# Node pass of a graph layer: on GpSimd the gather of aggregated rows is issued before the second norm's operation instead of behind it

## The chip, the cores and the metric

The kernel runs on one core of one Trainium2 chip. Its five engines (TensorE or PE, VectorE or DVE, ScalarE or ACT, GpSimd or POOL, SyncE or SP) run rows of instructions of their own and meet only at semaphores. The metric is the device time of one execution in microseconds (us), the median of several runs.

## The reference, cut to what matters

Inputs are 50000 nodes of 768 numbers and 25000 edges, sorted by destination.

```python
x = x + gnn(layernorm(x), src, dst, W, attn_l, attn_r, W_res)
x = x + ffn(layernorm(x), ...)

def gnn(h, src, dst, ...):                 # 12 heads of 64
    ft = einsum('nhd,od->nho', h, W)
    e = leaky_relu(a1[src] + a2[dst])      # then a softmax over the edges of a node
    agg = segment_sum(alpha[:, :, None] * ft[src], dst)
    res = einsum('nhd,od->nho', h, W_res)
    return relu(agg + res)

def ffn(x, ...):                           # 768 -> 96 -> 768; six class tokens aside
    return gelu(x @ W1 + b1) @ W2 + b2
```

An edge pass computes `agg` for nodes that have edges, and a node pass computes everything that every node needs: first norm, residual product, sum with `agg`, relu, second norm, feed-forward.

## The kernel before

The edge pass (to about 1150 us) leaves rows of `agg` in a scratch tensor in HBM, `agg_scratch`, and for every node the number of its row in `row_scratch`; nodes without edges have a number out of bounds, which the gather skips. The change doesn't touch the edge pass.

The node pass handles 392 units of 128 nodes, one in each iteration t of a loop that is written out in full (two turns of 196 and a drain). Each engine has its own copy of the loop, and in iteration t each step works on a unit that lies a fixed lag behind: the constants L_BASE = 3, L_RES = 4, L_Y = 5, L_SQ = 6, L_N2 = 9, L_T2 = 10, L_UP = 12, L_DOWN = 14, L_OUT = 15. Within an iteration the order of the code is the order of the engine's row; between engines only semaphores order things. The steps:

- SyncE loads the rows of x (`in_x`), their numbers `nrow` and a transposed copy (`in_x_cols`), and stores the output.
- ScalarE takes sums for the first norm (L644, L682), L665 the square sum for the second norm, L656 `t_hi`, a copy of the transposed second norm out of PSUM, and gelu.
- GpSimd, iteration t: **base** (L554) writes minus mean times weight sums times r_n into a slot of `g_ring`, for unit t-3. **n2** (L566) writes the second norm of unit t-9 into one of two buffers. **gather** (L574) is an indirect DMA that copies the rows of `agg_scratch` of unit t-3 over base in the slot, for the nodes that have one. In every even iteration **r_n** (L582) follows, the inverse roots for two units, out of `ve_n` from VectorE.
- TensorE, iteration t: the transposes of n2 of unit t-10 (L711), the up product (L845), the down product (L857) and the residual product of unit t-4 (L866), which waits for y of unit t-5.
- VectorE, iteration t: output sum (L1176), **z1** (L1187) for unit t-5, which adds the gathered slot and waits for the gather's landing (`d_g`) and the residual product, **y** (L1192), `t_lo` (L1199) behind `t_hi`, and in even iterations `ve_n` (L1210 to L1212), which releases r_n.

So a pair of iterations on GpSimd has two base, two n2, two gathers and one r_n. Base of the next odd iteration waits for r_n (`s_rn`), and so does its n2; the gather waits for base of the same iteration (`s_base`) and for `nrow` (`d_x`). n2 also waits for the transposes of two units before (`s_tp2`). In the first iterations, 3 to 8, there is no n2 yet.

Of the kernel before, what the change touches and what calls it, by code (L numbers as in the profile page):

```python
# [18 lines left out]
PAIR = 2  # L19
U = 196  # L20
XR = 14
GR = 7
NT = -(-N_NODES // (P * U)) * U
# [8 lines left out]
EP = EC * P  # L32
# [22 lines left out]
L_BASE = 3  # L55
# [16 lines left out]
def turns(eng, n, drain):  # L72


    yield 0
    yield 1
    if n > 2:
        with eng.Fori(2, n) as b:
            yield b
    for b in range(drain):  # L80
        yield n + b


def settle(eng):

    eng.nop(nofuse=True)


def exists(t, n):

    return not isinstance(t, int) or 0 <= t < n


def at_least(eng, sem, value):

    if not isinstance(value, int) or value > 0:
        eng.wait_ge(sem, value)


def gnn_ffn_kernel(nc, x, x_cols, edges, dst_next, dst_prev, dst_ends, chunk_base, sel_heads,  # L100
# [9 lines left out]
    with ExitStack() as ctx:  # L110
        def sb(name, shape, dt=f32):
            return ctx.enter_context(nc.sbuf_tensor(name, shape, dt))

        def sem(name):
            return ctx.enter_context(nc.semaphore(name))


        agg_d = nc.dram_tensor("agg_scratch", [EP, D], f32).ap()
# [7 lines left out]
        def part(lo, *shape, rows=P):  # L126
            size = 1
            for s in shape:
                size *= s
            flat = arena[0:rows, lo:lo + size]  # L130
            if len(shape) == 2:
                return flat.rearrange("p (a b) -> p a b", b=shape[1])
            if len(shape) == 3:
                return flat.rearrange("p (a b c) -> p a b c", b=shape[1], c=shape[2])
            return flat
# [12 lines left out]
        g_ring = part(16128, GR, D)  # L148
# [94 lines left out]
        nrow = sb("nrow", [P, XR], i32)  # L243
# [101 lines left out]
        d_x = [sem(f"d_x{u}") for u in range(XR // PAIR)]  # L345
        d_out = [sem(f"d_out{u}") for u in range(XR // PAIR)]
        d_xt = [sem(f"d_xt{u}") for u in range(GR)]
        d_g = [sem(f"d_g{u}") for u in range(GR)]
# [4 lines left out]
        s_base = sem("s_base")  # L353
# [138 lines left out]
        @block.gpsimd  # L492
        def _(pool):
            pool.wait_ge(d_rowinit, 16)

            for b in turns(pool, NB, 1):
                for i in range(BODY):
                    c = BODY * b + i
                    k = i % G
                    if exists(c, EC):  # L500
                        e = i // G
                        if k == 0:
                            pool.wait_ge(s_es, 2 * b + e + 1)
                        at_least(pool, s_tr, NBLK * (c - BODY + 1))
                        settle(pool)
                        pool.indirect_dma_start(xs_ring[:, i, :], None, x,
                                                bass.IndirectOffsetOnAxis(e_slot[:, e, k, 0:1], 0)).then_inc(d_ge[i], 16)
                        at_least(pool, s_sc, c - BODY)
                        settle(pool)
                        pool.indirect_dma_start(xd_ring[:, i, :], None, x,  # L510
                                                bass.IndirectOffsetOnAxis(e_slot[:, e, k, 1:2], 0)).then_inc(d_ge[i], 16)
                        at_least(pool, s_sum, c - BODY - L_SUM + L_TR + 1)
                        settle(pool)
                        pool.indirect_dma_start(row_d, bass.IndirectOffsetOnAxis(e_slot[:, e, k, 2:3], 0),
                                                e_slot[:, e, k, 3:4], None, bounds_check=NP - 1, oob_is_err=False)\
                            .then_inc(d_scat[e], 16)
                    gp = 2 * b + (i - 11) // G
                    if k == 11 % G and exists(gp, NG):
                        w = (i - 11) // G % 2
                        pool.wait_ge(s_ve, gp + 1)  # L520
                        settle(pool)
                        pool.tensor_tensor(r_a[:, w, 0:2 * G:2], ve_a[:, w, 0:2 * G:2], half[:, 0:G], ALU.pow)\
                            .then_inc(s_rp, 1)
                    gq = 2 * b + (i - 12) // G
                    if k == 12 % G and exists(gq, NG):
                        w = (i - 12) // G % 2
                        pool.tensor_tensor(r_a[:, w, 1:2 * G:2], ve_a[:, w, 1:2 * G:2], half[:, 0:G], ALU.pow)\
                            .then_inc(s_rpd, 1)

            for u in range(AR):  # L530
                pool.wait_ge(d_agg[u], 16 * (EC // AR))
            pool.wait_ge(s_idx, 1)
            for n in range(2):
                pool.indirect_dma_start(o_first[:, n, :], None, agg_d,
                                        bass.IndirectOffsetOnAxis(idx_i[:, n:n + 1], 0)).then_inc(d_first, 16)
            pool.wait_ge(s_frow, NC)
            pool.wait_ge(d_last, 16)
            pool.wait_ge(d_first, 32)
            for n in range(2):
                pool.indirect_dma_start(agg_d, bass.IndirectOffsetOnAxis(idx_i[:, n:n + 1], 0),  # L540
                                        fix_rows[:, n, :], None).then_inc(d_fix, 16)
            pool.wait_ge(d_fix, 32)
            for b in turns(pool, NT // U, 1):
                for u in range(U):
                    t = b * U + u
                    tb_ = t - L_BASE
                    if exists(tb_, NT):
                        v = (u - L_BASE) % XR
                        w = (v // PAIR + 1) % (XR // PAIR)
                        g = (u - L_BASE) % GR  # L550
                        pool.wait_ge(s_rn, b * (U // PAIR) + (u - L_BASE) // PAIR + 1)
                        at_least(pool, s_z1, tb_ - GR + 1)
                        settle(pool)
                        pool.tensor_scalar(g_ring[:, g, :].rearrange("p (c f) -> p c f", f=P),  # L554
                                           csr_neg[:, None, :].to_broadcast([P, NC, P]),
                                           mv1[:, w, 2 * (v % PAIR):2 * (v % PAIR) + 1], r_n[:, w, v % PAIR:v % PAIR + 1],
                                           ALU.mult, ALU.mult).then_inc(s_base, 1)
                    ty = t - L_N2
                    if exists(ty, NT):
                        v = (u - L_N2) % XR  # L560
                        w = (v // PAIR + 4) % (XR // PAIR)
                        k = v % PAIR
                        pool.wait_ge(s_rn, b * (U // PAIR) + (u - L_N2) // PAIR + 4)
                        at_least(pool, s_tp2, ty - 1)
                        settle(pool)
                        pool.tensor_scalar(n2[:, v % 2, :], y_ring[:, v, :], nm_n[:, w, k:k + 1],  # L566
                                           r_n[:, w, PAIR + k:PAIR + k + 1], ALU.add, ALU.mult).then_inc(s_n2, 1)
                    if exists(tb_, NT):
                        v = (u - L_BASE) % XR
                        g = (u - L_BASE) % GR  # L570
                        pool.wait_ge(d_x[v // PAIR], 32 * (U // XR * b + (u - L_BASE) // XR + 1))
                        pool.wait_ge(s_base, tb_ + 1)
                        settle(pool)
                        pool.indirect_dma_start(g_ring[:, g, :], None, agg_d,  # L574
                                                bass.IndirectOffsetOnAxis(nrow[:, v:v + 1], 0),
                                                bounds_check=EP - 1, oob_is_err=False).then_inc(d_g[g], 16)
                    q = b * (U // PAIR) + u // PAIR
                    if u % PAIR == 0 and exists(q - 1, NQ + 3):
                        w = u // PAIR % (XR // PAIR)
                        pool.wait_ge(s_ven, q)  # L580
                        settle(pool)
                        pool.tensor_tensor(r_n[:, w, :], ve_n[:, w, :], half[:, 0:4], ALU.pow).then_inc(s_rn, 1)  # L582
# [728 lines left out]
```

## Time and profile before

| | us |
|---|---|
| median of 3 runs | 3027.69 |
| lowest, highest | 3019.7, 3028.32 |
| the profiled execution, its own time | 3026.71 |
| span of its instructions | 3024.9 |
| mean granted TensorE clock (share of full speed) | 0.975 |

The busy shares of the whole span are TensorE 92%, VectorE 86%, ScalarE 72%, GpSimd 70%. They mix an edge pass and a node pass; the node pass starts to write its steps at about 1250 us. The profile's engines are named PE (with PEld for its weight loads), DVE, ACT, POOL. A wait is put down to what came last by the profile, and where a row names an engine that had long been done, it was something else, as in the waits of base "for PE L711" of 0.2 us, which is the wait for its own r_n. DMA_INDIRECT on POOL is the issue of a gather; the time until the rows have landed is not part of it.

### The profile page before, as it was taken

The page shows a single profiled execution, that of the slowest core. Times are in us where ns is not written, and L with a number is a line of the kernel's source. Part 1 is how long each engine was busy: PE and PEld are TensorE (multiplying, and loading weights), DVE is VectorE, ACT ScalarE, POOL GpSimd, SP SyncE. Part 2 cuts the span into 40 slices and gives each one's busy share as a digit, 9 for nine tenths or more (in the row PEclk, how much of TensorE's full clock was granted, in tenths as well). Part 3 has the DMA queues.
Part 4 walks back from the last instruction along what each step waited for, and adds up shares of the span by engine and source line. Part 5 has one row for each costly group of instructions (what it writes and reads, how often), then busy time and mean ns, then how long its engine had stood idle before and what let it go on. Part 6 is the DMA issues. An engine that isn't in the chain of part 4 may idle for free. (4 is left out here: it accounts for less than half of the span.)

```text
span 3024.9 us, 67973 instructions
## 1 busy us (share of the span) xinstructions
PE 2794.6 (92%) x21300; PEld 2580.3 (85%) x21300; DVE 2601.7 (86%) x5435; ACT 2186.3 (72%) x4168; POOL 2123.3 (70%) x2027
## 2 busy tenths in 40 slices
PE   1989999999999995589999999999999999999998
PEld 1878888888888883488999999999989999999996
DVE  4678899999999976488999999999989999989995
ACT  0655566666666561388888888998988989989992
POOL 6755566666666720378888888888878888888882
PEclk9999999999999998599999999999999999999998
DMA  8999999888887733489888888888888888888873
GB/s 176 168 182 211 197 217 215 220 217 212 220 218 219 213 120 125 167 289 326 313 311 313 304 306 307 301 300 305 301 281 296 305 294 302 302 288 296 298 259 126
DMA packets 246631, 758.02 MB, mean 251 GB/s; under 512 B 78899, under 2 KB 81203, under 8 KB 246291
## 3 DMA queue, kind: packets, MB, share of 16 engines
q1 hardware_dynamic: 176644, 545.08, 51.2%
q0 software_dynamic: 69312, 209.33, 31.2%
q8 instruction: 123, 2.02, 0.3%
q14 instruction: 120, 0.98, 0.1%
q10 hardware_dynamic: 432, 0.62, 0.1%
HBM read 623.04 MB, written 232.17 MB: 283 GB/s over the span
## 5 line engine op out<-in xcount | busy, mean ns | idle before, releaser
L866 PE MATMUL ps<-wr_bd,arena 128*128 128x128 f32 x4704 | 608.1, 280 | 92.9 <-DVE arena L1192 85.3
L866 PEld LDWEIGHTS ps<-wr_bd,arena 128*128 128x128 f32 x4704 | 567.7, 194 | 113.5 <-issue 111.6
L1187 DVE SCALAR_TENSOR_TENSOR ps<-ps,r_n,arena 128x768 f32<-128x768 f32 x392 | 400.1, 1021 | 114.4 <-DMA arena<-agg_scratch,nrow 93.6
L574 POOL DMA_INDIRECT arena<-agg_scratch,nrow x392 | 438.9, 1120 | 77.6 <-issue 72.4
L656 ACT ACTIVATE t_hi<-ps 128x768 fp32r<-128x768 f32 x392 | 315.0, 804 | 176.3 <-PE ps L711 176.2
L554 POOL TENSOR_SCALAR arena<-csr_neg,mv,r_n 128x768 f32<-128x768 f32 x392 | 386.8, 987 | 50.6 <-PE ps L711 37.7
L613 ACT ACTIVATE arena<-ps 128x512 f32<-128x512 f32 x588 | 312.1, 594 | 138.5 <-PE ps L728 100.4
L1192 DVE SCALAR_TENSOR_TENSOR arena<-ps,arena 128x768 f32<-128x768 f32 x392 | 375.3, 957 | 13.4
L566 POOL TENSOR_SCALAR arena<-arena,nm_n,r_n 128x768 f32<-128x768 f32 x392 | 383.4, 978 | 0.6 <-POOL r_n L582 0.4
L644 ACT ACTIVATE arena<-arena,mv 128x768 f32<-128x768 f32 x392 | 367.7, 938 | 12.7
L1199 DVE TENSOR_TENSOR t_lo<-ps,t_hi 128x768 fp32r<-128x768 f32 x392 | 373.7, 953 | 2.9 <-ACT t_hi L656 2.6
L1176 DVE TENSOR_TENSOR arena<-arena,ps 128x768 f32<-128x768 f32 x392 | 369.8, 943 | 6.3 <-PE ps L857 6.1
L665 ACT ACTIVATE arena<-arena,s_st 128x768 f32<-128x768 f32 x392 | 363.8, 928 | 9.8 <-DVE arena L1192 9.8
L845 PE MATMUL ps<-t_hi,w_hi 128*96 128x256 f32 x1176 | 361.0, 307 | 0.0
L728 PE MATMUL ps<-ident,arena 128*128 128x128 f32 x2352 | 296.2, 277 | 50.9 <-issue 49.7
L582 POOL TENSOR_TENSOR r_n<-ve_n,half 128x4 f32<-128x4 f32 x199 | 205.8, 1034 | 187.7 <-DVE ve_n L1212 187.1
L728 PEld LDWEIGHTS ps<-ident,arena 128*128 128x128 f32 x2352 | 275.3, 143 | 71.3 <-issue 52.6
L510 POOL DMA_INDIRECT arena<-in_x,e_slot x196 | 190.7, 973 | 198.5 <-PE ps L774 111.0
L845 PE MATMUL ps<-t_lo,w_hi 128*96 128x256 f32 x1176 | 329.8, 280 | 0.0
L845 PE MATMUL ps<-t_hi,w_lo 128*96 128x256 f32 x1176 | 328.7, 280 | 0.0
L682 ACT ACTIVATE arena<-arena 128x768 f32<-128x768 f32 x392 | 326.0, 832 | 0.5
L711 PE MATMUL ps<-ident,arena 128*128 128x128 f32 x2352 | 323.2, 274 | 1.3 <-POOL arena L566 0.8
(201 smaller groups left out, 6556.7 us busy)
## 6 DMA issues: line engine op xcount, KB each, us to landing
arena<-in_x SPq DMA_DIRECT2D x196, 768.0 KB
arena<-in_x_cols SPq DMA_DIRECT2D x392, 384.0 KB
out<-arena SPq DMA_DIRECT2D x195, 768.0 KB, 5.6
agg_scratch<-arena SPq DMA_DIRECT2D x196, 384.0 KB
arena<-in_x,e_slot POOLq DMA_INDIRECT x392
arena<-agg_scratch,nrow POOLq DMA_INDIRECT x392
row_scratch<-e_slot POOLq DMA_INDIRECT x196
nrow<-row_scratch SPq DMA_DIRECT2D x196, 1.0 KB
```

The source lines that it names most:

```text
L554: pool.tensor_scalar(g_ring[:, g, :].rearrange("p (c f) -> p c f", f=P), csr_neg[:, None, :].to_broadcast([P, NC, P]), mv1[:, w, 2 * (v % ...
L566: pool.tensor_scalar(n2[:, v % 2, :], y_ring[:, v, :], nm_n[:, w, k:k + 1], r_n[:, w, PAIR + k:PAIR + k + 1], ALU.add, ALU.mult).then_inc( ...
L574: pool.indirect_dma_start(g_ring[:, g, :], None, agg_d, bass.IndirectOffsetOnAxis(nrow[:, v:v + 1], 0), bounds_check=EP - 1, oob_is_err=Fa ...
L644: nc.scalar.activation(junk[:, 0, :], x_ring[:, v, :], ACT.Square, bias=mv1[:, w, 2 * k:2 * k + 1], scale=-1.0, accum_out=q_st[:, w, k:k + ...
L665: nc.scalar.activation(junk[:, 1, :], y_ring[:, v, :], ACT.Square, bias=s_st[:, w, k:k + 1], scale=-float(D), accum_out=q_st[:, w, 2 + k:3 ...
L728: last = nc.tensor.transpose(ps[:, k, m % 4 * P:(m % 4 + 1) * P], src[:, v, m % NC * P:(m % NC + 1) * P], ident[:])
L845: last = nc.tensor.matmul(ps[0:HID, 6 + v, 0:PAIR * P], w[:, i, :], h[:, i, :], start=(i == 0 and n == 0), stop=(i == NC - 1 and n == 2))
L866: last = nc.tensor.matmul(pair(1)[:, i * P:(i + 1) * P], xt_ring[:, g, i * P:(i + 1) * P], wr_bd[:], start=True, stop=True)
L1176: V.tensor_tensor(y_ring[:, v, :], y_ring[:, v, :], pair(2), ALU.add).then_inc(s_o, 1)
L1187: V.scalar_tensor_tensor(pair(1), pair(1), r_n[:, w, k:k + 1], g_ring[:, g, :], ALU.mult, ALU.add).then_inc(s_z1, 1)
L1192: V.scalar_tensor_tensor(y_ring[:, v, :], pair(1), 0.0, x_ring[:, v, :], ALU.max, ALU.add, accum_out=s_st[:, w4, k:k + 1]).then_inc(s_y, 1)
L1199: V.tensor_tensor(t2_lo[:, v, :, f], pair(0).rearrange("p (c n) -> p c n", c=NC), t2_hi[:, v, :, f].bitcast(f32), ALU.subtract).then_inc(s ...
```

## The change

The six lines of code of the gather move up, from behind n2 to ahead of it. Nothing else changes. What was L574 (the gather) becomes L564, and n2 moves from L566 to L575.

```diff
                     if exists(tb_, NT):
                         ...
                         pool.tensor_scalar(g_ring[:, g, :].rearrange("p (c f) -> p c f", f=P),
                         ...
                                            ALU.mult, ALU.mult).then_inc(s_base, 1)
+                    if exists(tb_, NT):
+                        v = (u - L_BASE) % XR
+                        g = (u - L_BASE) % GR
+                        pool.wait_ge(d_x[v // PAIR], 32 * (U // XR * b + (u - L_BASE) // XR + 1))
+                        pool.wait_ge(s_base, tb_ + 1)
+                        settle(pool)
+                        pool.indirect_dma_start(g_ring[:, g, :], None, agg_d,
+                                                bass.IndirectOffsetOnAxis(nrow[:, v:v + 1], 0),
+                                                bounds_check=EP - 1, oob_is_err=False).then_inc(d_g[g], 16)
                     ty = t - L_N2
                     if exists(ty, NT):
                         ...
                         pool.tensor_scalar(n2[:, v % 2, :], y_ring[:, v, :], nm_n[:, w, k:k + 1],
                                            r_n[:, w, PAIR + k:PAIR + k + 1], ALU.add, ALU.mult).then_inc(s_n2, 1)
-                    if exists(tb_, NT):
-                        ...
-                        pool.indirect_dma_start(g_ring[:, g, :], None, agg_d,
-                        ...
```

On GpSimd, at the seam between the iterations without n2 and the first one with it, before:

```order
194 L554 TENSOR_SCALAR arena<-csr_neg,mv,r_n 128x768 [waits s_rn]
195 L574 DMA arena<-agg_scratch,nrow 128x768 [waits d_x2,s_base]
196 L582 TENSOR_TENSOR r_n<-ve_n,half 128x4 [waits s_ven]
197 L554 TENSOR_SCALAR arena<-csr_neg,mv,r_n 128x768 [waits s_rn]
198 L566 TENSOR_SCALAR arena<-arena,nm_n,r_n 128x768 [waits s_rn]
199 L574 DMA arena<-agg_scratch,nrow 128x768 [waits d_x3,s_base]
200 L554 TENSOR_SCALAR arena<-csr_neg,mv,r_n 128x768 [waits s_rn,s_z1]
```

and of the changed kernel, in the same place:

```order
194 L554 TENSOR_SCALAR arena<-csr_neg,mv,r_n 128x768 [waits s_rn]
195 L564 DMA arena<-agg_scratch,nrow 128x768 [waits d_x2,s_base]
196 L582 TENSOR_TENSOR r_n<-ve_n,half 128x4 [waits s_ven]
197 L554 TENSOR_SCALAR arena<-csr_neg,mv,r_n 128x768 [waits s_rn]
198 L564 DMA arena<-agg_scratch,nrow 128x768 [waits d_x3,s_base]
199 L575 TENSOR_SCALAR arena<-arena,nm_n,r_n 128x768 [waits s_rn]
200 L554 TENSOR_SCALAR arena<-csr_neg,mv,r_n 128x768 [waits s_rn,s_z1]
```

Without n2 (rows 194 and 195) the order base, gather is the same in both; from row 198 on gather and n2 have changed places.

On GpSimd, a pair of iterations once all steps stand there, from the base of an odd iteration to the r_n of the even one, before:

```order
204 L554 TENSOR_SCALAR arena<-csr_neg,mv,r_n 128x768 [waits s_rn,s_z1]
205 L566 TENSOR_SCALAR arena<-arena,nm_n,r_n 128x768 [waits s_rn,s_tp2]
206 L574 DMA arena<-agg_scratch,nrow 128x768 [waits d_x4,s_base]
207 L554 TENSOR_SCALAR arena<-csr_neg,mv,r_n 128x768 [waits s_rn,s_z1]
208 L566 TENSOR_SCALAR arena<-arena,nm_n,r_n 128x768 [waits s_rn,s_tp2]
209 L574 DMA arena<-agg_scratch,nrow 128x768 [waits d_x4,s_base]
210 L582 TENSOR_TENSOR r_n<-ve_n,half 128x4 [waits s_ven]
```

and of the changed kernel:

```order
204 L554 TENSOR_SCALAR arena<-csr_neg,mv,r_n 128x768 [waits s_rn,s_z1]
205 L564 DMA arena<-agg_scratch,nrow 128x768 [waits d_x4,s_base]
206 L575 TENSOR_SCALAR arena<-arena,nm_n,r_n 128x768 [waits s_rn,s_tp2]
207 L554 TENSOR_SCALAR arena<-csr_neg,mv,r_n 128x768 [waits s_rn,s_z1]
208 L564 DMA arena<-agg_scratch,nrow 128x768 [waits d_x4,s_base]
209 L575 TENSOR_SCALAR arena<-arena,nm_n,r_n 128x768 [waits s_rn,s_tp2]
210 L582 TENSOR_TENSOR r_n<-ve_n,half 128x4 [waits s_ven]
```

In each iteration the gather stands directly behind the base that it waits for, and n2 between it and the next base or r_n. The rows of the other engines are the same.

## Rows read from the trace of the kernel before

**Rows 1.** Page, costliest groups: busy us, mean ns | idle us before them, releaser.

```profile
L1187 DVE SCALAR_TENSOR_TENSOR ps<-ps,r_n,arena 128x768 f32<-128x768 f32 x392 | 400.1, 1021 | 114.4 <-DMA arena<-agg_scratch,nrow 93.6
L574 POOL DMA_INDIRECT arena<-agg_scratch,nrow x392 | 438.9, 1120 | 77.6 <-issue 72.4
```

**Rows 2.** Waits, 1278.88 to 2959.5 us: us in total, times, longest us.

```profile
POOL r_n L582 <- DVE ve_n L1212: 172.2, 187, 5.0
...
DVE ps L1187 <- DMA arena<-agg_scratch,nrow: 88.7, 98, 4.8
...
PE ps L866 <- DVE arena L1192: 65.9, 76, 4.8
```

**Rows 3.** Busy time by stretch, from the first n2 to the last gather.

```profile
core 0: us, PE busy (x) PEld busy (x) DVE busy (x) ACT busy (x) POOL busy (x), PEclk, DMA share, GB/s
1278.88:2959.50 1680.62, 1606.72 (x12676) 1538.06 (x12676) 1529.71 (x2694) 1489.60 (x3072) 1385.77 (x1350) 0.99 0.87 299
```

**Rows 4.** Timeline of POOL, mid node pass: start us, us, instruction, [idle before].

```profile
1997.78 1.09 POOL L574 DMA_INDIRECT arena<-agg_scratch,nrow  x1 [0.17 <-issue]
1999.65 1.04 POOL L582 TENSOR_TENSOR r_n<-ve_n,half 128x4 f32<-128x4 f32 x1 [0.78 <-DVE ve_n L1212]
2000.89 0.99 POOL L554 TENSOR_SCALAR arena<-csr_neg,mv,r_n 128x768 f32<-128x768 f32 x1 [0.21 <-PE ps L711]
2001.87 0.98 POOL L566 TENSOR_SCALAR arena<-arena,nm_n,r_n 128x768 f32<-128x768 f32 x1
2003.02 1.14 POOL L574 DMA_INDIRECT arena<-agg_scratch,nrow  x1 [0.17 <-issue]
2004.21 0.98 POOL L554 TENSOR_SCALAR arena<-csr_neg,mv,r_n 128x768 f32<-128x768 f32 x1
2005.19 0.97 POOL L566 TENSOR_SCALAR arena<-arena,nm_n,r_n 128x768 f32<-128x768 f32 x1
2006.33 1.11 POOL L574 DMA_INDIRECT arena<-agg_scratch,nrow  x1 [0.17 <-issue]
2008.74 1.03 POOL L582 TENSOR_TENSOR r_n<-ve_n,half 128x4 f32<-128x4 f32 x1 [1.31 <-DVE ve_n L1212]
```

**Rows 5.** Timeline of POOL in the iterations before n2 begins.

```profile
1258.88 1.09 POOL L574 DMA_INDIRECT arena<-agg_scratch,nrow  x1 [0.89 <-issue]
1260.00 1.05 POOL L582 TENSOR_TENSOR r_n<-ve_n,half 128x4 f32<-128x4 f32 x1
1261.23 0.98 POOL L554 TENSOR_SCALAR arena<-csr_neg,mv,r_n 128x768 f32<-128x768 f32 x1 [0.18 <-POOL r_n L582]
1263.07 1.14 POOL L574 DMA_INDIRECT arena<-agg_scratch,nrow  x1 [0.85 <-POOL arena L554]
1264.26 0.98 POOL L554 TENSOR_SCALAR arena<-csr_neg,mv,r_n 128x768 f32<-128x768 f32 x1
1266.09 1.11 POOL L574 DMA_INDIRECT arena<-agg_scratch,nrow  x1 [0.84 <-issue]
1267.45 1.04 POOL L582 TENSOR_TENSOR r_n<-ve_n,half 128x4 f32<-128x4 f32 x1 [0.26 <-DVE ve_n L1212]
```

**Rows 6.** Timeline of DVE, mid node pass.

```profile
2005.48 1.03 DVE L1187 SCALAR_TENSOR_TENSOR ps<-ps,r_n,arena 128x768 f32<-128x768 f32 x1 [0.88 <-DMA arena<-agg_scratch,nrow]
...
2007.42 0.95 DVE L1199 TENSOR_TENSOR t_lo<-ps,t_hi 128x768 fp32r<-128x768 f32 x1
...
2009.36 1.02 DVE L1187 SCALAR_TENSOR_TENSOR ps<-ps,r_n,arena 128x768 f32<-128x768 f32 x1
```

**Rows 7.** Timeline of PEld and ACT, mid node pass.

```profile
1999.86 0.69 PEld L711 LDWEIGHTS ps<-ident,arena 128*128 128x128 f32 x6
...
2000.82 0.82 ACT L656 ACTIVATE t_hi<-ps 128x768 fp32r<-128x768 f32 x1 [0.63 <-PE ps L711]
...
2003.96 0.69 PEld L711 LDWEIGHTS ps<-ident,arena 128*128 128x128 f32 x6
```

## What I expect of the change

> **What bounds the kernel now.** I read four views: the groups of the page, for what is long and what stands idle ahead of it; the waits of the node pass, for who waits for whom; the timeline of GpSimd (POOL), for how its instructions follow one another; and the same stretch on VectorE (DVE), ScalarE (ACT) and TensorE (PE). In the groups the reader is to see that z1 (L1187) is idle most often for the gather, and that the gather has an idle of its own [rows 1]. In the waits: GpSimd waits 172.2 us for VectorE at r_n, so GpSimd has slack today; VectorE waits 88.7 us in 98 places for a gather to land; TensorE waits 65.9 us for y (L1192), behind z1 [rows 2].
>
> The stretch in which base, n2 and gather all stand is iterations 9 to 394: 386 iterations, 193 pairs (r_n comes once a pair). It lasts 1680.62 us [rows 3], so **8.71 us a pair**. TensorE alone would need less: with no wait, the transposes of two iterations stand 4.10 us apart (1999.86 and 2003.96), 8.20 us a pair [rows 7]. The rest is a loop through the gather. The second gather of a pair starts 6.68 us after r_n (1999.65 to 2006.33) [rows 4], is needed at a z1 two iterations on, and from the start of z1 to the r_n behind it are 3.26 us (2005.48 to 2008.74) [rows 4, 6]. Two pairs must hold 6.68, the time L from gather start to landing, and 3.26. Where z1 waited, at 2005.48, its gather had started at 1997.78: L = 7.70 us less the release [rows 4, 6]. Two pairs of 8.71 ask for an L of 7.5, so landing time of the second gather and the 8.20 of TensorE share the bound. The first gather of a pair isn't the late one: it starts at 2003.02 and its z1, at 2009.36, shows no wait [rows 4, 6].
>
> **What the change does to GpSimd's row.** Instructions, waits and sizes stay; only the order within an iteration turns. Before, while n2 runs for 0.98 us, the gather's wait for s_base and its preparation run beneath it, and 0.17 us behind n2 it starts: 1.15 us after base ends [rows 4]. After, nothing lies between base and gather. The trace shows that case: in the first iterations n2 isn't there yet, and the gather stands right behind its base. There the idle time is **0.85 and 0.84 us** (1263.07 and 1266.09), and so in every pair before n2 begins [rows 5]. The same instruction with the same waits, so I take 0.84. The nearest other row is the 0.21 between r_n and a base that waits for it [rows 4]; it is my lower bound, and r_n and base are both compute operations, so it is the farther one. The upper is 1.15, if the gather doesn't start sooner at all; both gaps at that price would make the pair 9.82 and add 214 + 10 us, 3251. Since the gap behind base is the same instruction and lies at 0.84 to 0.89 in all rows of this kind [rows 5], the ends are kept as rivals and the range goes by 0.81 to 0.89.
>
> The Trainium skill, "DMA: Bandwidth & Descriptors", section "Anatomy of one DMA — SWDGE (gpsimd) path", speaks for a short gap: dispatch by the sequencer is put at about 50 ns, descriptor generation is called small, and most of a DMA's fixed time is laid to its completion. By that the gather would start almost at base's end and issuing it first would be a gain; its result is the first rival below. The 0.84 us between base and gather in this trace speaks against it.
>
> The new pair, from start to start:
> - r_n to base 1.24 (1999.65 to 2000.89) [rows 4]
> - base to gather 1.84 (1261.23 to 1263.07) [rows 5]
> - gather to n2 1.19, the price of gather to base (1263.07 to 1264.26) [rows 5], both waiting for semaphores long satisfied
> - n2 to base 0.98, as base to n2 today [rows 4]
> - base to gather 1.83 (1264.26 to 1266.09) [rows 5]
> - gather to n2 1.12 (as to r_n, 1258.88 to 1260.00) [rows 5]
> - n2 to r_n 0.98, plus 0.02 if the queue isn't seamless
>
> Sum **9.20 us**, with GpSimd never idle but for the gaps. A second way: without n2, r_n 1260.00 to r_n 1267.45 is 7.45 us, 0.26 of it waiting for VectorE, so 7.19 [rows 5]; two n2 of 0.98 make 9.15. Since 9.20 is above 8.71, the 0.9 us that GpSimd waits at r_n today is eaten up and it becomes the bound. A pair grows by 0.49 us; 193 of them are **95 us**. Startup before iteration 9 and the drain behind iteration 394 keep their order and cost nothing more.
>
> **What else is late then.**
> The gathers: the first of a pair starts 3.08 us after r_n instead of 3.37, 0.3 earlier, where there was slack. The second, the one waited for, starts 7.08 after r_n instead of 6.68: 0.4 later. For it the change does not do what its name says, since n2 of the iteration before and two gaps now lie ahead of it. But a longer pair gives more time: 2 x 9.20 - 7.08 - 3.26 = 8.06 us for landing, against L = 7.70 in the typical late case. So most waits of z1 fall away or stay without effect; what remains are landings beyond 8.06. The 98 waits have a mean of 0.91 and a longest of 4.8 us [rows 2], so a few reach beyond. I take 10 us for them (an estimate), bounds 0 and 45, half of today's sum. DMA gets relief: its share of 0.87 [rows 3] becomes 0.82 if the same bytes take 9.20 us a pair.
>
> n2 is later: its end moves from 3.20 us after r_n (1999.65 to 2002.85) to 5.25, by 2.05. The transposes on it start at 2003.96, a cushion of 1.11 [rows 4, 7]. So TensorE will wait for n2 by about 1 us once a pair, where today it almost never does. Does that close a longer loop? r_n to end of n2 5.25, release 0.05, transposes to t_hi 0.96 (1999.86 to 2000.82), t_hi 0.82, release 0.05, t_lo to r_n 1.32 (2007.42 to 2008.74) [rows 4, 6, 7]: 8.45 us a pair, below 9.20. So TensorE's waits show, and GpSimd's own row sets the time. The n2 of the second iteration ends 3.93 us behind the first, less than TensorE's 4.10, and isn't waited for.
>
> Against the profiled run's own time, 3026.7 us: 3026.7 + 95 + 10 = 3132. The median shown is 1 us above the profiled run: **3133 us**.
>
> **Rivals.**
> Faster: *the gap between base and gather is short.* At 0.20 instead of 0.84 the pair on GpSimd is 9.20 - 1.28 = 7.92, below TensorE's 8.20; the second gather starts 5.80 after r_n, and the gather loop asks (7.5 + 5.80 + 3.26)/2 = 8.28. Then 193 x (8.28 - 8.71) = -83: 2945 us. It decides at a gap of 0.6 us, where the row on GpSimd is 8.71. The rule named above would give this; for it speaks only that r_n to base takes 0.21, against it every gather without n2 ahead of it. Chance 0.05.
>
> No change: *the gaps are partly covered*, about 0.6 each, because the preparation can overlap the base operation when the queue is full, and landings gain what n2 costs. In the rows without n2 the gather is just as free to be prepared early, and isn't. 3020 to 3036 us; chance 0.03.
>
> Slower still: *the loops add up,* or the gap is the upper bound. The second gather, 0.4 later, lands in a worse stretch of the bulk loads that SyncE issues, and z1 then holds up r_n while GpSimd has no slack to catch up in. Were today's waits all paid on top of the new pair, 95 + 88.7 = 184: 3211 us; half of them, 3170. For it: landing times differ much from pair to pair; against: DMA is less loaded and the landing has 8.06 us. Chance of beyond the forecast's own range 0.10.
>
> **Numbers.** Forecast 0.82, 3133 us, by itself 3110 (pair of 9.15, no residue: 3027 + 85) to 3185 (both gaps at 0.89, so a pair of 9.30, and 45 of residue: 3027 + 114 + 45). The range of 8 in 10 is that one, opened at the low end by a few us to 3105 for a gap a little below 0.84 (0.81 takes off 12). Slower by over 0.3% 0.92, within 0.3% 0.03, faster by over 0.3% 0.05; 0.3%, 9 us, is about what a measurement of this kernel can tell from no change.
>
> **What would show it.** Right: GpSimd's idle ahead of the gather goes from 0.17 to about 0.84 in all pairs, 320 us in total; r_n's wait for VectorE falls from 172 us to under 30; r_n to r_n is 9.2 in nearly every pair instead of swinging; TensorE waits for n2 (L711 for the n2 line) some 190 times, about 1 us each; the waits of z1 for the gather shrink or end without effect; TensorE's clock in the stretch stays near the 0.99 of before [rows 3]. Wrong: a gap well below 0.6 there, or r_n still waiting for VectorE in most pairs, which would mean that another loop than GpSimd's own row sets the time; a pair well above 9.3 with waits of z1 above 1 us would be the piling-up.

## The result and the profile after

The changed kernel takes **3176.65 us** (median of 4 runs, 3170.1 to 3179.44), the kernel before in the same comparison 3023.69 us (4 runs): a ratio of **1.0504**, 95% interval 1.0474 to 1.0534. The forecast was 3133 us, 3105 to 3185: slower, as said, but by 153 us where 109 (3133 against 3024) were forecast. The profiled execution took 3170.1 us, 143 more than that of before.

The groups of the changed kernel, as in [rows 1] but with up to three releasers, and VectorE's three small operations for r_n (busy us, mean ns | idle before, releasers):

```profile
L1187 DVE SCALAR_TENSOR_TENSOR ps<-ps,r_n,arena 128x768 f32<-128x768 f32 x392 | 398.3, 1016 | 32.8 <-PE ps L866 18.0 <-DMA arena<-agg_scratch,nrow 14.4
L564 POOL DMA_INDIRECT arena<-agg_scratch,nrow x392 | 438.9, 1120 | 348.5 <-issue 205.6 <-PE ps L711 136.0 <-DVE ps L1187 4.3
L1212 DVE TENSOR_SCALAR ve_n<-q_st 128x2 f32<-128x2 f32 x199 | 151.4, 761 | 0.0
L1210 DVE TENSOR_SCALAR ve_n<-q_st 128x2 f32<-128x2 f32 x199 | 102.2, 513 | 9.0 <-DMA agg_scratch<-arena,idx_i 6.9 <-ACT arena L644 2.1
L1211 DVE TENSOR_SCALAR nm_n<-s_st 128x2 f32<-128x2 f32 x199 | 31.8, 160 | 0.0
```

The gather itself costs what it did, 1120 ns, but GpSimd is idle ahead of it for 348.5 us instead of 77.6: the engines named behind the arrow had long been done; the idle time is the gap between base and gather. And two operations on 128x2 elements take 761 and 513 ns. Of the kernel before, the same two lines read:

```profile
L1212 DVE TENSOR_SCALAR ve_n<-q_st 128x2 f32<-128x2 f32 x199 | 32.8, 165 | 0.0
L1210 DVE TENSOR_SCALAR ve_n<-q_st 128x2 f32<-128x2 f32 x199 | 31.9, 160 | 9.0 <-DMA agg_scratch<-arena,idx_i 6.9 <-ACT arena L644 2.1
```

The waits of the changed kernel in the stretch of its 193 pairs, and the stretch's busy time, answer to [rows 2, 3]:

```profile
PEld ps L711 <- POOL arena L575: 223.6, 192, 3.7
...
PE ps L711 <- POOL arena L575: 187.1, 191, 3.5
...
POOL r_n L582 <- DVE ve_n L1212: 38.1, 191, 2.2
...
DVE ps L1187 <- DMA arena<-agg_scratch,nrow: 9.5, 13, 2.9
```

```profile
1273.80:3103.70 1829.90, 1635.97 (x12680) 1542.57 (x12680) 1714.75 (x2696) 1509.84 (x3072) 1387.67 (x1350) 0.99 0.80 274
```

TensorE now waits for n2 once a pair, z1's waits for the gather have fallen from 88.7 to 9.5 us, r_n waits for VectorE 38.1 us instead of 172.2, and the stretch lasts 1829.9 instead of 1680.6 us: 9.48 us a pair. One pair on GpSimd, and the end of it on VectorE (timelines):

```profile
2007.04 1.04 POOL L582 TENSOR_TENSOR r_n<-ve_n,half 128x4 f32<-128x4 f32 x1 [0.18 <-DVE ve_n L1212]
2008.29 0.99 POOL L554 TENSOR_SCALAR arena<-csr_neg,mv,r_n 128x768 f32<-128x768 f32 x1 [0.20 <-POOL r_n L582]
2010.12 1.14 POOL L564 DMA_INDIRECT arena<-agg_scratch,nrow  x1 [0.85 <-issue]
2011.31 0.98 POOL L575 TENSOR_SCALAR arena<-arena,nm_n,r_n 128x768 f32<-128x768 f32 x1
2012.28 0.97 POOL L554 TENSOR_SCALAR arena<-csr_neg,mv,r_n 128x768 f32<-128x768 f32 x1
2014.09 1.09 POOL L564 DMA_INDIRECT arena<-agg_scratch,nrow  x1 [0.83 <-PE ps L711]
2015.23 1.00 POOL L575 TENSOR_SCALAR arena<-arena,nm_n,r_n 128x768 f32<-128x768 f32 x1
2016.41 1.04 POOL L582 TENSOR_TENSOR r_n<-ve_n,half 128x4 f32<-128x4 f32 x1 [0.18 <-DVE ve_n L1212]
```

```profile
2014.98 0.49 DVE L1210 TENSOR_SCALAR ve_n<-q_st 128x2 f32<-128x2 f32 x1
2015.37 0.16 DVE L1211 TENSOR_SCALAR nm_n<-s_st 128x2 f32<-128x2 f32 x1
2015.44 0.81 DVE L1212 TENSOR_SCALAR ve_n<-q_st 128x2 f32<-128x2 f32 x1
```

From r_n to r_n are 9.37 us (2007.04 to 2016.41). GpSimd's row looks as forecast but for the last step: r_n doesn't follow n2 but waits 0.18 us for ve_n, whose last operation ends at 2016.25, right behind n2 at 2016.23. That was not in the sum. This is the usual pair and not only this one: of the r_n between 1300 and 2900 us 161 of 169 start 0.18 us late behind such a long last operation.

### The profile page after: what moved, and what is told of

Its sections match the earlier page's. It is cut to its first block and busy times, and to the rows that moved or that the text cites. A ratio compares the mean times of both kernels' runs of the same rounds, so it can differ in the third digit from the quotient of the medians.

```text
span 3168.3 us, 67973 instructions
## 1 busy us (share of the span) xinstructions
PE 2820.1 (89%) x21300; PEld 2582.2 (82%) x21300; DVE 2786.6 (88%) x5435; ACT 2206.1 (70%) x4168; POOL 2124.1 (67%) x2027
## 5 line engine op out<-in xcount | busy, mean ns | idle before, releaser
L564 POOL DMA_INDIRECT arena<-agg_scratch,nrow x392 | 438.9, 1120 | 348.5 <-issue 205.6
L866 PE MATMUL ps<-wr_bd,arena 128*128 128x128 f32 x4704 | 600.4, 278 | 26.6 <-DVE arena L1192 26.1
L711 PE MATMUL ps<-ident,arena 128*128 128x128 f32 x2352 | 335.1, 279 | 187.7 <-POOL arena L575 187.1
L711 PEld LDWEIGHTS ps<-ident,arena 128*128 128x128 f32 x2352 | 260.4, 141 | 227.2 <-POOL arena L575 223.6
L575 POOL TENSOR_SCALAR arena<-arena,nm_n,r_n 128x768 f32<-128x768 f32 x392 | 386.0, 985 | 22.0 <-POOL r_n L582 0.6
L728 PE MATMUL ps<-ident,arena 128*128 128x128 f32 x2352 | 295.4, 276 | 50.6 <-issue 49.6
L728 PEld LDWEIGHTS ps<-ident,arena 128*128 128x128 f32 x2352 | 274.5, 143 | 70.6 <-issue 51.8
```

The source lines that it names most:

```text
L564: pool.indirect_dma_start(g_ring[:, g, :], None, agg_d, bass.IndirectOffsetOnAxis(nrow[:, v:v + 1], 0), bounds_check=EP - 1, oob_is_err=Fa ...
L711: last = nc.tensor.transpose(dst[:, c * P:(c + 1) * P], src[:, c * P:(c + 1) * P], ident[:])
L728: last = nc.tensor.transpose(ps[:, k, m % 4 * P:(m % 4 + 1) * P], src[:, v, m % NC * P:(m % NC + 1) * P], ident[:])
L866: last = nc.tensor.matmul(pair(1)[:, i * P:(i + 1) * P], xt_ring[:, g, i * P:(i + 1) * P], wr_bd[:], start=True, stop=True)
```

## The experiments

**Theory A**: there are loops of two kinds, GpSimd's own row (now 9.20 us of its own, plus 0.18 by which ve_n is held until n2 ends) and one through the landing of the second gather; what is longer sets the time. Its rivals are that each moved gather costs the same wherever it stands (theory C), that only GpSimd's row counts (theory B), and that ve_n is late for another reason. Ratios are against the kernel before on the same chip; where a mean over pairs is given, it is over the pairs between 1300 and 2900 us of the trace.

### The change in half of the iterations

In odd iterations only (the gather behind r_n and base), `e1_odd_only`:

```diff
+                    if u % PAIR == 1 and exists(tb_, NT):
+                        ...                              # the gather, ahead of n2
                     ty = t - L_N2
                     ...
-                    if exists(tb_, NT):
+                    if u % PAIR == 0 and exists(tb_, NT):
                         ...
```

> The gather directly behind base only in odd iterations (the first of a pair, right behind r_n); in even iterations n2 stays ahead of it, as before. Theory A (two loops: GpSimd's own row, and the one through the landing of the second gather): GpSimd's row is 8.50 us a pair, but the second gather starts 7.38 us after r_n instead of 6.68, so the gather loop asks for (7.5 + 7.38 + 3.26)/2 = 9.07 us: 193 pairs x 0.36 = 70 us, some 3095 us; z1 waits for the second gather in most pairs. Theory B (only GpSimd's row counts): 8.50 is below the 8.71 of before, so no change, 3015 to 3035 us. Theory C (each moved gather costs the same): half of the whole change's 152, some 3100 us, with GpSimd busy rather than VectorE waiting.

Measured: 3045.46 us, ratio 1.0119 (1.0095 to 1.0143), some 36 us on the 3006 that the kernel before takes on that chip, where theory A had 70 and about 3095 us: a miss by half. The other half, `e2_even_only`, with 1 and 0 exchanged:

> The gather directly behind base only in even iterations (the second of a pair); odd iterations as before. Theory A: row 8.67 us a pair with 0.18 for ve_n held up until n2 ends, second gather 0.3 earlier (6.39 us after r_n), so the gather loop asks for only 8.58: 3020 to 3045 us, waits of z1 for the gather clearly below the 88.7 us of before. Theory C (each moved gather costs the same): some 3100 us. In all theories ve_n (the last of the three small VectorE operations) takes 0.8 us instead of 0.16, if it is held up by the n2 that runs beside it.

Measured: 3037.34 us, ratio 1.0099 (1.0078 to 1.0119). This lies within its forecast, and the waits of z1 fell as expected, to 56.8 us in 77 places. So each half costs about 1% and both together 5%: theory C (half of 152 each) falls, and so does theory B, by which e1 costs nothing. The timeline of e1 on GpSimd:

```profile
2003.74 1.03 POOL L591 TENSOR_TENSOR r_n<-ve_n,half 128x4 f32<-128x4 f32 x1 [0.74 <-DVE ve_n L1221]
...
2011.08 1.10 POOL L583 DMA_INDIRECT arena<-agg_scratch,nrow  x1 [0.17 <-issue]
2012.31 1.03 POOL L591 TENSOR_TENSOR r_n<-ve_n,half 128x4 f32<-128x4 f32 x1
```

Its row needs 8.57 us without a wait (forecast 8.50), below the 8.71 of before, and its second gather starts 7.34 us behind r_n, as forecast. But a pair lasts 8.91 us on average and not the 9.07 of the gather loop; z1 waits 43.2 us in 66 places, fewer than in the kernel before and not in most pairs. The L of 7.5 put into the loop was too long here. In e2 the row is 8.71 (2005.75 to 2014.46 on r_n, with the 0.18 in it) and a pair lasts 8.90 on average. So theory A's rule that the longer loop sets the time is not exact: both runs lie above GpSimd's row. What the pairs show is that the short ones are gone. In the kernel before more than half of them (95 of 182) last less than 8.55 us and a tenth 9.66 or more, so that a late landing can be made up. In e1 none lasts less than 8.56 and a tenth 9.48 or more; in e2 these are 8.69 and 9.16. That this is the whole reason is argued: e1 also has waits of TensorE for n2 that the kernel before hardly had (67.6 us in 133 places), and no run takes the two apart.

In e2 ve_n's last operation was 0.8 us long too, as had been expected, though only in 86 of 179 pairs:

```profile
2013.16 0.35 DVE L1219 TENSOR_SCALAR ve_n<-q_st 128x2 f32<-128x2 f32 x1
2013.42 0.16 DVE L1220 TENSOR_SCALAR nm_n<-s_st 128x2 f32<-128x2 f32 x1
2013.50 0.81 DVE L1221 TENSOR_SCALAR ve_n<-q_st 128x2 f32<-128x2 f32 x1
```

In e1, where the second n2 stands ahead of the gather and is long over, the r_n at 2012.31 follows the gather without a wait.

### What the 0.84 us ahead of the gather are

`e4_gather_lag4`, the gather of the unit before the one whose base was just written:

```diff
+L_GAT = 4
...
-                    if exists(tb_, NT):
+                    tg_ = t - L_GAT
+                    if exists(tg_, NT):
...
-                        pool.wait_ge(s_base, tb_ + 1)
+                        pool.wait_ge(s_base, tg_ + 1)
```

> As the changed kernel, but the gather directly behind base of unit t-3 is that of unit t-4, whose base was written an iteration before (lag 4 instead of 3), so its wait is long satisfied. Theory A (the 0.84 us of idle ahead of the gather are preparation that can start only when base has ended, because of the wait): with the wait satisfied the idle is 0.2 us or less, as behind n2. Rival (preparation never overlaps the operation just ahead of the gather): 0.84 again. The time says nothing for the change, since z1 gets its rows an iteration later: by the gather loop 3.3 to 4 us more a pair, 3650 to 3850 us.

Measured in a single run: 3338.2 us, and on GpSimd:

```profile
2004.62 0.99 POOL L555 TENSOR_SCALAR arena<-csr_neg,mv,r_n 128x768 f32<-128x768 f32 x1 [0.21 <-POOL r_n L584]
2005.78 1.14 POOL L566 DMA_INDIRECT arena<-agg_scratch,nrow  x1 [0.17 <-POOL arena L555]
```

Right behind a base the idle is 0.17, not 0.84, in 305 of 306 gathers between 1300 and 2900 us. So GpSimd can prepare a gather beneath the operation ahead of it, and it is the wait for *that* operation that puts the preparation into the open. The forecast of the time was a miss: 3338 instead of 3650 to 3850; z1 waits 354.9 us in 194 places, and TensorE's granted clock in this stretch was 0.94 instead of 0.99. Here too the landings came sooner than the 7.5 us put in: 3.9 us on average for the gather of an odd iteration, 5.6 for that of an even one (how this is read stands below).

### Why ve_n is long

`e3_after_ve_early`: the changed kernel with VectorE's three operations moved from behind t_lo to ahead of it.

```diff
+                    q = b * (U // PAIR) + u // PAIR
+                    if u % PAIR == 0 and exists(q - 1, NQ + 3):
+                        ...                              # ve_n, nm_n, ve_n
                     tl = t - L_T2
                     ...                                  # t_lo
-                    q = b * (U // PAIR) + u // PAIR
-                    ...
```

> The changed kernel, with VectorE's three small operations of ve_n ahead of t_lo instead of behind it, so that they run while GpSimd doesn't compute. Theory A (in the changed kernel ve_n is held until n2 ends on GpSimd, and r_n starts 0.18 us late in each pair): the three operations fall back to 0.16 us each, r_n follows n2 at once, r_n to r_n is 9.20 us, 193 x 0.15 to 0.18 = 30 to 35 us less, 3140 to 3150 us. Rival (ve_n comes late because t_lo, and TensorE's wait for n2 before it, come late, and its length is only a way of recording a wait): with ve_n ahead of t_lo the same gain would come, but without the operations on VectorE being short where they now meet base or the gather. Rival (the 9.37 us are GpSimd's own): no change, 3170 to 3180 us.

Measured: 3120.14 us, ratio 1.0377 (1.0354 to 1.0399) against 1.0504 for the changed kernel: 1.3% of 3024, some 38 us back. The two intervals leave 27 to 50, so this agrees with the 30 to 35 expected (3140 to 3150 had been named for a chip on which the kernel before takes 3024; here it took 3006). In the pair shown r_n follows n2 at once, and from r_n to r_n are 9.15 us (2005.07 to 2014.22), GpSimd's row as forecast:

```profile
2004.11 0.98 POOL L575 TENSOR_SCALAR arena<-arena,nm_n,r_n 128x768 f32<-128x768 f32 x1
2005.07 1.03 POOL L582 TENSOR_TENSOR r_n<-ve_n,half 128x4 f32<-128x4 f32 x1
...
2014.22 1.04 POOL L582 TENSOR_TENSOR r_n<-ve_n,half 128x4 f32<-128x4 f32 x1
```

That the operations would all fall back to 0.16 us was not borne out: the last one is still long in 45 of 172 pairs. In a like number, 45, r_n is late; in the other 127 it isn't. This doesn't yet tell whether the operations were held by GpSimd. `e9_after_accum` leaves them at their place and only changes their form (and leaves out the factors 1/D and 1/D^3, so the output is another):

```diff
-                        V.tensor_scalar(ve_n[:, w, 0:2], q_st[:, w, 0:2], 1.0 / D, EPS, ALU.mult, ALU.add)
+                        V.tensor_scalar(ve_n[:, w, 0:2], q_st[:, w, 0:2], D * EPS, None, ALU.add, ALU.add,
+                                        accum_out=acc_n[:, w, 0:1])
                         V.tensor_scalar(nm_n[:, w, :], s_st[:, w, :], -1.0 / D, None, ALU.mult)
-                        V.tensor_scalar(ve_n[:, w, 2:4], q_st[:, w, 2:4], 1.0 / D ** 3, EPS, ALU.mult, ALU.add)\
+                        V.tensor_scalar(ve_n[:, w, 2:4], q_st[:, w, 2:4], D * EPS, None, ALU.add, ALU.add,
+                                        accum_out=acc_n[:, w, 1:2])\
```

> The changed kernel; the two operations of ve_n are at their old place, in the form that also writes out an accumulator, and leave out the factors 1/D and 1/D^3 (so r_n is another number; sizes, waits and order stay). Theory A (the plain form of these operations can't run beside GpSimd's n2, and this is what holds them for 0.8 us): in the accumulating form they take 0.2 us or so although n2 runs beside them, r_n follows n2 without the 0.18 us, and the time falls as with ve_n ahead of t_lo, by 20 to 40 us. Rival (their length in the record is a wait for data or for n2's data, whatever their form): still 0.8 us, r_n again 0.18 us behind n2, no change of time.

Measured: 3123.99 us, ratio 1.0369 (1.0337 to 1.04), the same as e3 within the intervals. VectorE and GpSimd at the same time:

```profile
2009.24 0.99 POOL L576 TENSOR_SCALAR arena<-arena,nm_n,r_n 128x768 f32<-128x768 f32 x1
2010.21 1.03 POOL L583 TENSOR_TENSOR r_n<-ve_n,half 128x4 f32<-128x4 f32 x1
```

```profile
2008.97 0.14 DVE L1211 TENSOR_SCALAR_CACHE_REDUCE ve_n<-q_st 128x2 f32<-128x2 f32 x1
...
2009.04 0.42 DVE L1213 TENSOR_SCALAR nm_n<-s_st 128x2 f32<-128x2 f32 x1
2009.37 0.14 DVE L1214 TENSOR_SCALAR_CACHE_REDUCE ve_n<-q_st 128x2 f32<-128x2 f32 x1
```

The last operation, which ran 0.81 us beside n2, now runs 0.14 us, beside the n2 that starts at 2009.24, and r_n follows n2 without a wait in 163 of 172 pairs. The one in between, nm_n, kept the plain form and is now long, 0.42 us here and 0.72 in the pair before. So it is the plain form, and GpSimd running beside it, that stretches them.

The Trainium skill, "SBUF — State Buffer", section "Who interferes with whom", has a rule for this: GpSimd shares a pair of ports with some VectorE operations, among which `tensor_scalar` can be in some of its modes but not in its accumulating form, and the one that comes second is blocked until the other is through. The trace agrees for the last operation, with 0.81 against 0.14 us and an end 0.02 us behind n2's. It does not agree everywhere. In the changed kernel the plain operation in between took 0.16 us beside n2 in every pair (2015.37 above, inside the n2 of 2015.23). And the first long one, at 2014.98, as nm_n in e9, does not end with n2 but some 0.2 us after n2 has begun; it began beside the gather's issue. No run here explains these two.

`e6_even_ve_early` joins e2 and the shift of ve_n (the two diffs above together):

> The gather directly behind base in even iterations only, and ve_n ahead of t_lo. Theory A: the 0.18 us by which r_n followed the end of n2 go, GpSimd's row is 8.49 us a pair, and the gather loop has the same 0.95 us less over two pairs, so the row decides: 8.5 to 8.6 a pair, 2985 to 3005 us, faster than the same order without it (3037) by 35 to 50 us. It should be slower than the kernel before with the same shift of ve_n, since there GpSimd's row is 7.9 us.

Measured: 3039.81 us, ratio 1.007 (1.0044 to 1.0097): a miss. It is 0.3% better than e2, where 35 to 50 us were forecast, and the intervals overlap. The shift doesn't help where VectorE is ahead: its three operations then begin at 2007.13, the n2 of the even iteration starts at 2007.26, and the last one is held again:

```profile
2007.26 0.99 POOL L575 TENSOR_SCALAR arena<-arena,nm_n,r_n 128x768 f32<-128x768 f32 x1
```

```profile
2007.47 0.81 DVE L1214 TENSOR_SCALAR ve_n<-q_st 128x2 f32<-128x2 f32 x1
```

It ends at 2008.28, 0.03 us behind n2, and r_n starts 0.18 us late. So it goes in 122 of 180 pairs. What counts is not the place in VectorE's row but what GpSimd runs at that moment. The shift also has a price of its own: TensorE now waits for t_lo, 40.1 us in 140 places.

### What bounded the kernel before

`e10_short_store`: the kernel before, its store cut to 64 of 768 columns (the rest of the output is left out).

```diff
-                        sp.dma_start(out_v[ds(q, 1), lo:P].rearrange("q p k c -> p (q k) c"),
-                                     y_ring[lo:P, v:v + PAIR, :]).then_inc(d_out[v // PAIR], 16)
+                        sp.dma_start(out_v[ds(q, 1), lo:P, :, 0:D // 12].rearrange("q p k c -> p (q k) c"),
+                                     y_ring[lo:P, v:v + PAIR, 0:D // 12]).then_inc(d_out[v // PAIR], 16)
```

> The kernel before; the output store writes only the first 64 of 768 columns (the rest of the output is left out), so that a third of the bulk bytes of a pair is missing while queues, waits and engines stay. Theory A (the second gather lands late because it shares the DMA engines with the store and the loads issued around it, and this waiting is what keeps the kernel before from TensorE's 8.20 us a pair): the waits of z1 for the gather fall from some 90 us to under 30, 8.2 to 8.3 us a pair, 60 to 90 us less than before. Rival (a gather needs its 7 us by itself, or TensorE's waits come from elsewhere): waits and time within 15 us of before.

Measured: 2955.88 us, ratio 0.9806 (0.9774 to 0.9837), 57 us less, just short of the 60 to 90 expected; the waits of z1 in that stretch are a quarter of [rows 2]:

```profile
POOL r_n L582 <- DVE ve_n L1212: 101.6, 181, 3.5
...
DVE ps L1187 <- DMA arena<-agg_scratch,nrow: 22.9, 37, 3.2
```

So most of z1's waiting comes with the bytes of the store, and not because a gather takes 7 us by itself. `e5_before_ve_early` shortens the loop at another point, with the same shift of ve_n as e3, in the kernel before:

> The kernel before, with VectorE's three small operations of ve_n ahead of t_lo. Theory A (the kernel before is bound in part by the loop r_n, second gather, landing, z1, ve_n, r_n over two pairs): t_lo, 0.95 us, falls out of the piece from z1 to r_n (3.26 us), so two pairs need 0.95 us less and a pair goes from 8.71 towards TensorE's 8.20: 8.25 to 8.5 us, 40 to 90 us less, so 2915 to 2965 us on a chip where the kernel before takes 3006. Rival (the time of the kernel before is set by how fast the rows land and TensorE's own work, r_n is not in a loop): no change, 2997 to 3015 us.

Measured: 2990.28 us, ratio 0.9909 (0.9882 to 0.9937): the loop is there, but 27 us came back and not 40 to 90. z1 still waits 61.6 us in 78 places. A pair of rows shows where the rest went; z1 at 2013.56 waits for the gather of 2005.37, which had started 8.19 us before:

```profile
2005.37 1.10 POOL L574 DMA_INDIRECT arena<-agg_scratch,nrow  x1 [0.17 <-issue]
```

```profile
2013.56 1.03 DVE L1187 SCALAR_TENSOR_TENSOR ps<-ps,r_n,arena 128x768 f32<-128x768 f32 x1 [0.76 <-DMA arena<-agg_scratch,nrow]
```

In the kernel before it was 7.70 [rows 4, 6]. Two rows prove little, but the trace also holds the moments at which the semaphore of each gather is raised. The last one recorded is taken as the landing; some are missing from the traces, so that a mean may be a little too small. Where z1 waited, it starts 0.12 us behind it. Means in us, from the start of the gather, the first of a pair being that of the odd iteration (e7 and e8 are described below):

| | a pair lasts | landing of the first gather | of the second |
|---|---|---|---|
| before | 8.72 | 3.9 | 6.8 |
| after | 9.49 | 3.5 | 5.9 |
| e1 | 8.91 | 3.8 | 6.5 |
| e5 | 8.57 | 4.1 | 7.4 |
| e10 (short store) | 8.33 | 3.5 | 5.8 |
| e7 | 8.91 | 4.8 | 7.1 |
| e8 | 8.31 | 4.1 | 6.4 |

In before, after, e1 and e5 the second gather takes longer to land the faster the pairs come. Without most of the store it lands a microsecond sooner although the pairs come faster still, and in e8, with another order on GpSimd, it lands sooner too, so the length of a pair is not all. And the landing is not one number: in the kernel before a tenth of the second gathers land within 6.0 us and a tenth take 7.8 or more. The 7.5 of the gather loop is a late one, not the usual one.

### A version that beats both

`e7_pairwise` covers the preparation of both gathers: over a pair r_n, base, n2, base, gather, gather, n2. Against the changed kernel:

```diff
-                    if exists(tb_, NT):
+                    if u % PAIR == 1 and exists(tb_, NT):
                         ...                              # base of t-3
+                    ty = t - L_N2
+                    if u % PAIR == 1 and exists(ty, NT):
+                        ...                              # n2 in the odd iteration
+                    tb_ = t - L_BASE2                    # L_BASE2 = 2
+                    if u % PAIR == 1 and exists(tb_, NT):
+                        ...                              # base of t-2
+                    tb_ = t - L_BASE
                     if exists(tb_, NT):
                         ...                              # gather of t-3
                     ty = t - L_N2
-                    if exists(ty, NT):
+                    if u % PAIR == 0 and exists(ty, NT):
                         ...                              # n2 in the even iteration
```

> GpSimd's order over a pair of iterations: r_n, base, n2, base, gather, gather, n2. The base of the even iteration is written in the odd one, so that base and n2 cover the preparation of both gathers, and the second gather starts about 5.85 us after r_n (before: 6.68), the first 4.35 (before: 3.37, with slack). Theory A: GpSimd's row is about 7.9 us, the gather loop has 0.8 us less over two pairs: 8.3 to 8.5 us a pair, 40 to 80 us less than before, 2925 to 2965 us. Rival (two gathers close together land later, the first one now as late as the second): no gain or a loss, with z1 waiting in both iterations, 3000 to 3040 us. The idle between the two gathers tells what preparation costs behind another gather.

Measured: 3053.4 us, ratio 1.0119 (1.0086 to 1.0152), 1.2% slower: the rival. z1 waits 109.3 us in 95 places, and now mostly in the iteration that had slack. `e8_pairwise_ve_early` adds the shift of ve_n:

> The pairwise order and ve_n ahead of t_lo together. Theory A: the gather loop over two pairs asks for less than 8 us a pair, so TensorE's own 8.20 sets it: 8.20 to 8.35 us a pair, 2905 to 2940 us, waits of z1 for the gather under 20 us in total. Rival (TensorE's waits for y have another source than the gather): no better than the better one of the two alone.

Measured: **2942.35 us, ratio 0.9745 (0.972 to 0.977)**, 2.5% faster than the kernel before and 7% faster than the changed one, if 2 us above the 2905 to 2940 expected. Its pairs mostly follow each other at TensorE's pace, r_n to r_n 8.20 us here and 8.31 on average, with 0.4 us of idle left on GpSimd and 20.7 us of waits for gathers in all:

```profile
2006.16 1.03 POOL L606 TENSOR_TENSOR r_n<-ve_n,half 128x4 f32<-128x4 f32 x1 [0.38 <-DVE ve_n L1229]
2007.39 0.99 POOL L555 TENSOR_SCALAR arena<-csr_neg,mv,r_n 128x768 f32<-128x768 f32 x1 [0.21 <-POOL r_n L606]
2008.37 0.99 POOL L567 TENSOR_SCALAR arena<-arena,nm_n,r_n 128x768 f32<-128x768 f32 x1
2009.34 0.99 POOL L577 TENSOR_SCALAR arena<-csr_neg,mv,r_n 128x768 f32<-128x768 f32 x1
2010.50 1.15 POOL L588 DMA_INDIRECT arena<-agg_scratch,nrow  x1 [0.17 <-issue]
2011.95 1.01 POOL L588 DMA_INDIRECT arena<-agg_scratch,nrow  x1 [0.30 <-issue]
2013.01 0.99 POOL L599 TENSOR_SCALAR arena<-arena,nm_n,r_n 128x768 f32<-128x768 f32 x1
2014.36 1.04 POOL L606 TENSOR_TENSOR r_n<-ve_n,half 128x4 f32<-128x4 f32 x1 [0.37 <-DVE ve_n L1229]
```

Its two parts alone give -0.9% (e5) and +1.2% (e7), together -2.5%. That the gather loop falls below TensorE's 8.20 only with both would fit this, and is argued. Why e7 alone is slower than the kernel before, although its second gather starts 0.9 us sooner (5.78 behind r_n), its trace shows in part. Its first gather starts 1.0 us later than before (4.33 behind r_n instead of 3.37) and takes 4.8 us to land instead of 3.9, so it is there some 2 us later; z1 waits for it in 73 pairs (7 in the kernel before), and for the second one in 22 (90 before). Why the gathers take longer to land at that place isn't settled.

## Why the prediction was right, and where it was short

- **The gap of 0.84 us between base and gather**, read off the iterations without n2 [rows 5]: right, 0.83 to 0.85 in the timeline of after, and e4 shows its cause. It is what made the change slower: 348.5 us of idle instead of 77.6, where some 320 were forecast.
- **GpSimd's row of 9.20 us takes over as the bound**: right. In e3, in the pairs in which nothing else holds it, the row is 9.15, the second way of the prediction's sum (7.19 + 1.96). The first gather starts 3.08 us behind r_n, the second 7.05, both as worked out: the gather that was waited for did go out later and not sooner.
- **n2 to r_n, "0.98, plus 0.02 if the queue isn't seamless"**: this is the term that was too small. It measured 1.00 + 0.18, and r_n waited in 191 pairs, 38.1 us in all. The prediction counted the time at which ve_n's data is ready, by a loop of 8.45 us, and didn't ask what GpSimd is doing when VectorE's small operations run. Before, they mostly ran while GpSimd sat idle at r_n; without that idle they ran into the gather's issue and n2. In the profile this is 9.37 instead of 9.20 us a pair, 33 us for 193 of them; e3 and e9 give it 1.3%, 27 to 50 us. So it is most of the 44 by which the forecast was short.
- **The residue of 10 us**: too small by about as much again, and for another reason than forecast. The stretch is 1829.9 us; 193 pairs of 9.37 are 1808; 22 are left. They are not late landings. The idle ahead of the 386 gathers is some 343 us (348.5 without the six first), where 0.84 each would be 324: 19 us of it are longer gaps. Every 16th gather has one of 1.13 to 1.15 us, about as many others lie near 1.0, and three gathers that stand 107 apart wait 3.44 or 3.45 us, as this one, at 1784 us. The kernel before has three of about 2.5 us too. No row shows what causes them.

```profile
1783.98 0.97 POOL L554 TENSOR_SCALAR arena<-csr_neg,mv,r_n 128x768 f32<-128x768 f32 x1
1788.40 1.09 POOL L564 DMA_INDIRECT arena<-agg_scratch,nrow  x1 [3.45 <-issue]
```

- **Waits of z1 mostly vanish**: right, 9.5 us of 88.7. **TensorE waits for n2 some 190 times, about 1 us each**: right, 191 times, 187.1 us. DMA share 0.82 forecast, 0.80 measured, and TensorE's clock stays at 0.99.
- **r_n's wait for VectorE under 30 us**: 38.1; r_n waits for VectorE in nearly every pair, which the prediction had named as a sign that another loop sets the time. It isn't one: ve_n ends when n2 ends, so GpSimd's own row still sets the pace, with 0.18 us added to it.
- **The gather loop with a fixed L of 7.5 us**: right in kind (e5, e10), wrong as a constant. It gave 9.07 us a pair for e1 (8.91 measured), far too much for e4 and 40 to 90 us for e5 (27 measured). The second gather of the kernel before lands after 6.8 us on average; this grew to 7.4 in e5 and fell to 5.9 in the changed kernel.
- **The range of 3105 to 3185**: that 3177 lies in it is in part luck. Its upper end was made of gaps of 0.89 us and 45 us of late landings. The gaps were 0.84 and late landings cost z1 9.5 us; the room left for them was filled by the 0.18 at r_n and the longer gaps, which the prediction did not have.

The rival with the short gap and the one of no change are out by the gap itself. The piling-up of gather waits isn't what made the time longer than forecast, since z1 waits 9.5 us for gathers instead of 88.7.

## What to carry to other kernels

An operation that stands between a producer and an instruction that waits for it on the same engine may be the cover for that instruction's preparation. Here, issuing the waiting one first let it start 0.3 us sooner behind its producer and opened 0.84 us of idle, 386 times. Look in the trace for a place where the cover is missing already (here the first iterations of the loop); it has the price of the new order. And when an engine's last idle goes, ask which small operation of a neighbour used to run in it.

## What the hardware showed unexpectedly

- `tensor_scalar` on VectorE over 128x2 elements took 0.81 us instead of 0.16 beside a GpSimd operation, and ended within 0.03 us of it; in the accumulating form it took 0.14. A plain one just ahead of it, beside the same GpSimd operation, took 0.16.
- A gather directly behind another one has 0.30 us of idle, directly behind an operation that it doesn't wait for 0.17, behind the one that it waits for 0.84.
- The second gather's landing isn't a constant: 6.8 us from its start on average in the kernel before, 7.4 with pairs of 8.57 us, 5.9 with pairs of 9.49, and 5.8 when the store writes a twelfth of its columns.
